# Last stage of a graph-attention kernel: x in chunks behind the first sums, VectorE's steps regrouped, the projection's bias as a matmul

## The reference, cut to what matters

```python
att = _segment_softmax(score, edge_dst, n_nodes)[..., None]      # e / (sum of e + 1e-16)
out = jax.ops.segment_sum(value * att, edge_dst, num_segments=n_nodes)
out = out.reshape(n_nodes, H * VH)
return out @ w_proj + b_proj
...
x = x + _L0_gnn_ref(h, node_vec1, edge_weight1, edge_attr_32, src, dst, batch0, ...)
```

## Time and profile before

| | us |
|---|---|
| median of 3 runs (5342.77 to 5343.44) | 5342.91 |
| the profiled execution | 5343.49 |
| its span, first to last instruction | 5341.7 |
| last stage: first DMA issued | 5205.24 |
| first "den" of VectorE | 5232.42 |
| first finish starts | 5236.56 |
| last finish starts | 5336.25 |

### The profile page before, as it was taken

The page is one execution under the profiler, slowest core; times in us unless marked ns, Lnnn a source line. Parts: engine busy times, 40 slices in busy tenths (PEclk is TensorE's granted clock), DMA queues, the critical chain, the costliest instruction groups (busy, mean ns, idle before and its releaser), DMA issues. The chain is left out here.

```text
span 5341.7 us, 120270 instructions
## 1 busy us (share of the span) xinstructions
PE 5090.1 (95%) x34849; PEld 3951.6 (74%) x34849; DVE 4194.0 (79%) x8740; ACT 2107.5 (39%) x4768; POOL 3641.1 (68%) x3589
## 2 busy tenths in 40 slices
PE   3679999999999999999999999999999999999975
PEld 3557777777777777777777777777777777777764
DVE  5647788888888788888878888887888888887877
ACT  1434444444444444444443434444344444444421
POOL 2467777777777777777777777777777777777715
PEclk8689999999999999999999999999999999999965
DMA  5566676766667676766667676666767666676735
GB/s 148 149 168 188 183 191 181 192 183 188 189 182 191 179 194 183 190 187 185 187 182 192 181 192 187 187 187 183 191 180 194 184 189 187 183 191 183 191 70 145
DMA packets 1076171, 963.37 MB, mean 180 GB/s; under 512 B 188372, under 2 KB 911096, under 8 KB 1075199
## 3 DMA queue, kind: packets, MB, share of 16 engines
q1 hardware_dynamic: 945211, 716.69, 48.5%
q0 software_dynamic: 108784, 223.44, 16.4%
q10 hardware_dynamic: 21524, 15.49, 1.1%
HBM read 809.06 MB, written 149.13 MB: 179 GB/s over the span
## 5 line engine op out<-in xcount | busy, mean ns | idle before, releaser
L1037 POOL DMA_INDIRECT gath<-msg_src,idx x3328 | 3467.7, 1042 | 1361.3 <-issue 1016.7
L1184 ACT ACTIVATE h<-z_ps,b 128x256 f32<-128x256 f32 x832 | 394.7, 474 | 1853.4 <-PE z_ps L1242 1825.2
L1223 ACT ACTIVATE sil<-a_ps,ba 128x512 f32<-128x512 f32 x832 | 572.9, 689 | 981.0 <-PE a_ps L1339 962.2
L1283 PE MATMUL rad_ps<-wval,hot 128*128 128x136 f32 x6656 | 935.5, 285 | 23.1 <-DVE run L1145 23.0
L1344 PEld LDWEIGHTS v_ps<-wv,msgT 128*128 128x128 f32 x6656 | 874.7, 192 | 43.7 <-issue 0.5
L1339 PE MATMUL a_ps<-msgT,wa 128*128 128x512 f32 x1664 | 890.3, 617 | 8.7 <-DVE msgT L1155 8.6
L1344 PE MATMUL v_ps<-wv,msgT 128*128 128x128 f32 x6656 | 878.0, 275 | 0.0
L1283 PEld LDWEIGHTS rad_ps<-wval,hot 128*128 128x128 f32 x6656 | 852.2, 195 | 30.8 <-issue 30.7
L1111 DVE SCALAR_TENSOR_TENSOR rads<-rad_ps,b,ea_bc 128x512 f32<-128x512 f32 x832 | 624.4, 751 | 292.3 <-PE rad_ps L1257 285.1
L1155 DVE TENSOR_TENSOR msgT<-xT_ps,rads 128x512 f32<-128x512 f32 x832 | 575.7, 692 | 317.2 <-PE xT_ps L1323 297.4
L1167 DVE SCALAR_TENSOR_TENSOR sil<-a_ps,sil 128x512 f32<-128x512 f32 x832 | 571.7, 687 | 304.0 <-ACT sil L1223 289.6
(11 more groups left out here) (229 smaller groups left out, 4629.7 us busy)
## 6 DMA issues: line engine op xcount, KB each, us to landing
ea_bc<-ea_rows SPq DMA_DIRECT2D x832, 256.0 KB
win<-msg_dst SPq DMA_DIRECT2D x1664, 96.0 KB
sums<-run SPq DMA_DIRECT2D x832, 136.0 KB
rel_bc<-rel_rows SPq DMA_DIRECT2D x832, 128.0 KB
attr<-in_edge_attr_t SPq DMA_DIRECT2D x1664, 32.0 KB
gath<-msg_src,idx POOLq DMA_INDIRECT x3328
msg_dst<-dst_parts SPq DMA_DIRECT2D x98, 96.0 KB, 1.8
pen_g<-pen_rows SPq DMA_DIRECT2D x208, 32.1 KB
```

The source lines that it names most:

```text
L1037: pool.indirect_dma_start(gath[:, u, s], None, msg_src, bass.IndirectOffsetOnAxis(ap=idx[:, j // 8, at:at + 1], axis=0)).then_inc(s_gath[u ...
L1223: act.activation(sil[:, j % 8], a_ps[:, :], ACT.Silu, bias=ba[:, :]).then_inc(s_sil, 1)
L1283: last = pe.matmul(rad_ps[:, i, CE:CE + AW], lhsT=hot[:, j % 2, s], rhs=wval[:, j % 2, s].rearrange("p h k -> p (h k)"), start=(r == 0), s ...
```

## The change

Four things change in the last stage.

1. x is loaded in chunks between the sums: chunk 0 by SyncE's queue behind the sums of pairs 0 and 1, chunk c (1 to 6) by ScalarE's queue in its iteration q = 7(c - 1), behind the sums of pair q + 4 and ahead of the copy of pair q. Each group of loads uses one of three semaphores in turn.
2. VectorE's whole-chunk add of `bproj` goes, and with it the semaphore `rows_biased`. GpSimd's first add of a chunk waits for the chunk's load instead.
3. The projection's bias is added by TensorE: for each half of a pair one more matmul, a row of ones (1x128) times `bproj[0:1, :]` (1x128), starts the sum in PSUM that the projection ends.
4. VectorE's steps are regrouped. Iteration q now does den(q + 2), reciprocal(q + 1), mean(q) and share(q), finish(q - 2). The semaphore `mean_steps` counts two steps a pair, `reciprocal_steps` the other two. So the sums of pair q + 2 are wanted in iteration q.

```diff
@@ -1363,34 +1363,30 @@
             rows_x = tb("rows_x", [P, NB, C])
...
             den, share = tb("den", [P, S, 2, H]), tb("share", [P, S, 2])
+            ones_row = tb("ones_row", [1, P])
...
             s_in = [ts(f"sums_in{u}") for u in range(S)]
             s_x = [ts(f"rows_in{n}") for n in range(3)]
-            s_mean, s_T, s_Ts, s_mm, s_fin = ts("mean_steps"), ts("meanT_done"), ts("meanT_copied"), ts("projected"), ts("out_ready")
-            s_xb, s_bias, s_bw, s_out = ts("rows_biased"), ts("biases_added"), ts("bias_projected"), ts("out_stored")
-
-            def x_group(c):
-
-                return (0, 16) if c == 0 else (1, 32) if c < 3 else (2, 80)
+            s_inv, s_mean = ts("reciprocal_steps"), ts("mean_steps")
+            s_T, s_Ts, s_mm, s_fin = ts("meanT_done"), ts("meanT_copied"), ts("projected"), ts("out_ready")
+            s_bias, s_bw, s_out = ts("biases_added"), ts("bias_projected"), ts("out_stored")
 
             def load_x(eng, c):
                 if c < NB // CH - 1:
-                    eng.dma_start(rows_x[:, CH * c:CH * (c + 1)], x[P * CH * c:P * CH * (c + 1), :].rearrange("(b p) c -> p b c", p=P)).then_inc(s_x[x_group(c)[0]], 16)
+                    eng.dma_start(rows_x[:, CH * c:CH * (c + 1)], x[P * CH * c:P * CH * (c + 1), :].rearrange("(b p) c -> p b c", p=P)).then_inc(s_x[c % 3], 16)
                 else:
-                    eng.dma_start(rows_x[:, CH * c:NB - 1], x[P * CH * c:P * (NB - 1), :].rearrange("(b p) c -> p b c", p=P)).then_inc(s_x[2], 16)
-                    eng.dma_start(rows_x[0:tail, NB - 1], x[P * (NB - 1):N, :]).then_inc(s_x[2], 16)
+                    eng.dma_start(rows_x[:, CH * c:NB - 1], x[P * CH * c:P * (NB - 1), :].rearrange("(b p) c -> p b c", p=P)).then_inc(s_x[c % 3], 16)
+                    eng.dma_start(rows_x[0:tail, NB - 1], x[P * (NB - 1):N, :]).then_inc(s_x[c % 3], 16)
 
             def load_sums(eng, q, i):
                 u = q % S
                 last = eng.value_load(last_item[0:1, 2 * q + i:2 * q + i + 1], min_val=0, max_val=NI - 1)
-                need(eng, s_mean, 4 * (q - S + 1))
+                need(eng, s_mean, 2 * (q - S + 1))
                 eng.dma_start(agg[:, u, i].rearrange("p h k -> p (h k)"), sums[bass.ds(last, 1)].rearrange("o p c -> p (o c)")).then_inc(s_in[u], 16)
 
             @block.sync
             def _(sp):
-                load_x(sp, 0)
-
                 def store(c):
                     sp.wait_ge(s_fin, CH // 2 * (c + 1))
                     if c < NB // CH - 1:
@@ -1400,6 +1396,8 @@
                         sp.dma_start(out[P * (NB - 1):N, :], rows_x[0:tail, NB - 1]).then_inc(s_out, 16)
                 for q in range(NP):
                     load_sums(sp, q, 0)
+                    if q == 1:
+                        load_x(sp, 0)
                     if q % S == S - 2 and q > S:
                         store(q // S - 1)
                 store(NB // CH - 1)
@@ -1407,33 +1405,47 @@
 
             @block.gpsimd
             def _(pool):
-                pool.wait_ge(s_bw, 4)
+                pool.wait_ge(s_bw, 6)
                 for q in range(NP):
                     pair = rows_x[:, 2 * q:2 * q + 2]
-                    pool.wait_ge(s_mean, 4 * q + 4)
+                    pool.wait_ge(s_mean, 2 * q + 2)
                     pool.tensor_tensor(shared[:, q % 2], bias_out[:, :].unsqueeze(1).broadcast_to((P, 2, C)),
                                        share[:, q % S].unsqueeze(2).broadcast_to((P, 2, C)), ALU.mult).then_inc(s_bias, 1)
                     pool.wait_ge(s_bias, 2 * q + 1)
-                    pool.wait_ge(s_xb, q // (CH // 2) + 1)
+                    if q % (CH // 2) == 0:
+                        c = q // (CH // 2)
+                        pool.wait_ge(s_x[c % 3], 16 * (c // 3 + 1) if c < NB // CH - 1 else 16 * (c // 3 + 2))
                     pool.tensor_tensor(pair, pair, shared[:, q % 2], ALU.add).then_inc(s_bias, 1)
 
             @block.vector
             def _(dve):
-                dve.memset(rows_x[:, NB - 1], 0.0)
+                dve.memset(rows_x[:, NB - 1], 0.0).then_inc(s_bw, 1)
+                dve.memset(ones_row[:, :], 1.0).then_inc(s_bw, 1)
                 dve.tensor_copy(bias_in[:, :, :], bval[:, :, 1, :]).then_inc(s_bw, 1)
-                dve.wait_ge(s_bw, 3)
+                dve.wait_ge(s_bw, 5)
                 dve.tensor_copy(bias_out[:, :], PS[4][:, 0:C]).then_inc(s_bw, 1)
+
+                def den_at(q):
+                    return 2 * q if q > 1 else q + 1
+
+                def inverse_at(q):
+                    return 2 * q + 3 if q < NP - 1 else 2 * NP
+
+                def guard_den(q):
+                    dve.wait_ge(s_in[q % S], 32 * (q // S + 1))
+                    dve.tensor_scalar(den[:, q % S], agg[:, q % S, :, :, AH], 1e-16, None, ALU.add).then_inc(s_inv, 1)
+
+                def invert(q):
+                    dve.wait_ge(s_inv, den_at(q))
+                    dve.reciprocal(den[:, q % S], den[:, q % S]).then_inc(s_inv, 1)
 
                 def divide(q):
                     u = q % S
-                    dve.wait_ge(s_in[u], 32 * (q // S + 1))
+                    dve.wait_ge(s_inv, inverse_at(q))
                     need(dve, s_T, q - S + 1)
-                    dve.tensor_scalar(den[:, u], agg[:, u, :, :, AH], 1e-16, None, ALU.add).then_inc(s_mean, 1)
-                    dve.wait_ge(s_mean, 4 * q + 1)
-                    dve.reciprocal(den[:, u], den[:, u]).then_inc(s_mean, 1)
-                    dve.wait_ge(s_mean, 4 * q + 2)
                     dve.tensor_tensor(mean[:, u].rearrange("p i (h k) -> p (i h) k", h=H), agg[:, u, :, :, 0:AH].rearrange("p i h k -> p (i h) k"),
                                       den[:, u].rearrange("p i h -> p (i h)").unsqueeze(2).broadcast_to((P, 2 * H, AH)), ALU.mult).then_inc(s_mean, 1)
+                    need(dve, s_bias, 2 * (q - S) + 1)
                     dve.tensor_tensor(share[:, u], agg[:, u, :, 0, AH], den[:, u, :, 0], ALU.mult).then_inc(s_mean, 1)
 
                 def finish(q):
@@ -1442,12 +1454,14 @@
                     dve.wait_ge(s_bias, 2 * q + 2)
                     dve.tensor_tensor(pair, PS[2 + q % 2][:, 0:2 * C], pair, ALU.add).then_inc(s_fin, 1)
 
+                guard_den(0)
+                guard_den(1)
+                invert(0)
                 for q in range(NP):
-                    if q % (CH // 2) == 0:
-                        c = q // (CH // 2)
-                        chunk = rows_x[:, CH * c:CH * (c + 1)]
-                        dve.wait_ge(s_x[x_group(c)[0]], x_group(c)[1])
-                        dve.tensor_tensor(chunk, chunk, bproj[:, :].unsqueeze(1).broadcast_to((P, CH, C)), ALU.add).then_inc(s_xb, 1)
+                    if q + 2 < NP:
+                        guard_den(q + 2)
+                    if q + 1 < NP:
+                        invert(q + 1)
                     divide(q)
                     if q > 1:
                         finish(q - 2)
@@ -1456,28 +1470,30 @@
 
             @block.scalar
             def _(act):
-                act.wait_ge(s_bw, 2)
+                act.wait_ge(s_bw, 4)
                 act.activation(bias_t[:, :], PS[5][:, 0:P], ACT.Copy).then_inc(s_Ts, 1)
-                for c in range(1, NB // CH):
-                    load_x(act, c)
                 for q in range(4):
                     load_sums(act, q, 1)
                 for q in range(NP):
                     if q + 4 < NP:
                         load_sums(act, q + 4, 1)
+                    c = q // (CH // 2) + 1
+                    if q % (CH // 2) == 0 and c < NB // CH:
+                        need(act, s_bias, 2 * CH // 2 * (c - 3) + 2 if c > 2 else 0)
+                        load_x(act, c)
                     act.wait_ge(s_T, q + 1)
                     need(act, s_mm, q - S + 1)
                     act.activation(meanT[:, q % S].rearrange("p i c -> p (i c)"), PS[q % 2][:, 0:2 * P], ACT.Copy).then_inc(s_Ts, 1)
 
             @block.tensor
             def _(pe):
-                pe.wait_ge(s_bw, 1)
+                pe.wait_ge(s_bw, 3)
                 pe.transpose(PS[5][:, 0:P], bias_in[:, :, :].rearrange("p h k -> p (h k)"), ident[:, :]).then_inc(s_bw, 1)
                 pe.wait_ge(s_Ts, 1)
                 pe.matmul(PS[4][:, 0:C], lhsT=bias_t[:, :], rhs=wproj[:, :], start=True, stop=True).then_inc(s_bw, 1)
 
                 def turn(q):
-                    pe.wait_ge(s_mean, 4 * q + 3)
+                    pe.wait_ge(s_mean, 2 * q + 1)
                     need(pe, s_Ts, q if q > 1 else 0)
                     for i in range(2):
                         last = pe.transpose(PS[q % 2][:, i * P:(i + 1) * P], mean[:, q % S, i], ident[:, :])
@@ -1487,7 +1503,8 @@
                     pe.wait_ge(s_Ts, q + 2)
                     need(pe, s_fin, q - 1)
                     for i in range(2):
-                        last = pe.matmul(PS[2 + q % 2][:, i * C:(i + 1) * C], lhsT=meanT[:, q % S, i], rhs=wproj[:, :], start=True, stop=True)
```

(2 more changed lines are left out.)

## The result

The changed kernel takes **5382.5 us** (median of 4 runs, 5380.8 to 5385.1) against 5342.8 us before: ratio 1.0078, 95% interval 1.0066 to 1.0090. It is 40 us slower, where 14 us less were forecast, and outside the range.

The account below looks back on a forecast made before the run. Bound: VectorE and GpSimd taking turns, 1.85 us a pair, after a start waiting on loads. -12.9 - 16.8 + 0 + 2.4 + 1.0 + 12 = -14.3 us from 5343.49 gives 5329.2, median 5328.6; range 5312 to 5343.

Parts of the forecast that it names:

- Chunk adds: VectorE's whole-chunk bias adds go: 2.15 us saved at each of the 6 chunks behind chunk 0, -12.9 us.
- Start: Start of the last stage: first finish at about 5219.8 instead of 5236.56, behind sums 2, -16.8 us.
- Regrouping: VectorE's reordered steps: about 0.2 us a pair of its own work saved but hidden behind GpSimd, 0 us.
- Late sums: Sums wanted two pairs earlier, beside x and stores: den waits at pairs 13, 20, 27 and so on, +12 us.
- rival 2: TensorE stays at the half clock: every pair costs 2.66 us, late sums are covered, about 5352 us; chance 0.08.
- Tail: Behind the last mean, project(47) and project(48) are each 0.53 us longer, +1.0 us.
- Bias on TensorE: Two more fp32 matmuls per pair: 3 pairs at 2.66 us before the full clock holds at 1.33, +2.4 us.

Follow-up runs that it names:

- The best version: Changed kernel with one 128-row, 256-column bias matmul per pair, ScalarE's sums six pairs ahead, stores two pairs later, x loads moved: 5303.6 us, ratio 0.9927.

## Why the prediction was wrong

**Chunk adds, -12.9.** The 4.0 us intervals went, as forecast. Alone it is worth 10.3 us (5328.6 against 5318.3), since part of the adds' time had covered late sums.

**Start, -16.8.** Right in size and mechanism: -16.4, with sums 2 in use 5.5 us after their issue, behind chunk 0.

**Regrouping, 0.** Off by a little. I saw that the mean would be ready within 0.06 us of GpSimd's add and gave the turn to GpSimd; the mean gets it. I also wrote that it would make no difference then (1.84), having let the add end 0.4 later. It ends 0.25 later, the share ends with it, and the interval is 1.76: -4 to -6 us. The engines' taking turns, on which this rested, is what the rows show. The Trainium skill's rule (VectorE: DVE Perf Modes, on the DRAIN) that a semaphore costs nothing extra is not tested by any run here, since VectorE's own work was never the bound; the gain came by the order of the two engines, which the rule is silent on.

**Late sums, +12.** Right in size where it can be seen, 12.4 us in the run without bias matmul, and at the pairs that were named (13, 20, 27 and so on). But the forecast had one wait there, and from pair 13 to 41 there are two, at the pair before as well, besides one at pair 5 that it did not have; that the sum agrees is partly luck. In the changed kernel itself it is 0, as rival 2 said, because 3.32 us intervals cover it.

**Tail, +1.0.** The last two intervals took 6.2 us instead of 1.7, for the same reason as all the others: they too waited for TensorE.

**Bias on TensorE, +2.4.** This is the step that failed, twice: a cost that the term put at nothing, and a clock that it had rising after 3 pairs.

First the price of a pair. I took 0.27 us for a pass at the half clock from two starts 1.09 us apart. TensorE was not back to back there: its next transposes waited for this mean, which ended at 5236.03, and started at 5236.09.

```profile
5235.47 0.56 DVE L1435 TENSOR_TENSOR mean<-agg,den 128x256 f32<-128x256 f32 x1
```

A pass costs 0.215 us. That error alone made the pair too dear (2.66; all of one height, 2.15). Against it stands a cost that no row had: 4 steps between unlike heights at 0.29 us, 1.17 us a pair. I had priced a one-row weight load by its duration (308 ns, and the profile after has 308 for it too), and by duration it is right. What it costs is the overlap: it does not start beside the matmul in flight. The Trainium skill (TensorE: Matmul & The Clock Gate, on what each phase is for) says that weight loads are pulled ahead where the row groups do not conflict or where they go to a background buffer, and that the row count does not matter to a load's timing. The traces agree with the second sentence: 308 ns for one row, 310 for 128. On the first they show what it leaves open: a load of the same height as the matmul in flight was pulled ahead of it by 0.21 us, one of another height was not.

Then the clock. I took "no idle time at all" for what raises it. By the profile TensorE had none from the first finish on, for 158 us, and stayed at 0.50.

Together they make the interval TensorE's 3.32 instead of GpSimd's 1.76 to 1.85: 47 x 1.47 us = 69 us against the forecast's interval of 1.85. That is more than the net loss of 40 us, since the gains from the start and the chunk adds came. The two parts can be told apart by an estimate from measured intervals. The unlike steps are 47 x 1.17 = 55 us of the 69. With them gone and the clock still at the half, the interval would be 2.15 and the time about 5331 us, 12 us under the kernel before, if the sums are not late; the low clock alone is the other 14. So the step that I had put at nothing is the larger part. What the unlike steps cost in this stage at the full clock, no run shows.

I gave the slow clock 0.08 as rival 2, and gave it the wrong price, 2.66: at that price it would have been 5352. The same sum with 3.32 gives 5236.56 - 16.8 + 47 x 3.32 + 2.9 + 5.5 + 1.8 = 5386, against 5380.8 for the profiled execution, whose edge stage was 5.6 us shorter.

What should have warned me: the one row of evidence for a held full clock was of full-height matmuls only, while 20 us at 0.50 with TensorE busy for 15 said that this stage does not raise the clock easily. I laid that to the idle gaps of the chunk adds; the run without chunk adds and bias matmuls has none of them, only the waits for sums, and stood at 0.50 for 60 us at a time.

## What to carry to other kernels

Before adding a small matmul between large ones, ask what height it has: give it the full 128 rows (1/128 in each, or zeros below the first row). That took the same number of instructions and columns, and here it was the difference between 5382 and 5322 us. (One wide bias matmul instead of two ran only together with other moves; its own worth is not known.) When a stage is bound by two engines that take turns, move the instruction that decides which goes first, and look for the wait that takes over; when loads are wanted earlier, look at which bulk transfers they share the time with: issuing them sooner alone gained nothing here, issuing them sooner and moving x and the stores took the waits away.

## What the hardware showed that I had not expected

- A step between a 128-row fp32 matmul and a 1-row or 64-row one costs 0.29 us at the half clock; between equal heights it costs nothing. With 0, 2 and 4 such steps a pair took 2.13, 2.73 and 3.32 us.
- Four kernels with one-row bias matmuls (in turn with the projection, the same in the kernel before, grouped, 512 columns wide) and one with 64-row ones stayed at the half clock for 129 us or more with TensorE reported 100% busy. With 128 rows, even with 127 of them zero, the clock went to 1.0 within about 3 us of the first finish. In the edge stage 64-row matmuls stand among 128-row ones at the full clock.
- The best version kept the clock at 1.0 through its steady part with TensorE busy 15 of 20 us; the kernel before, busy 15 of 20, mostly had 0.50. PE's busy share is thus no guide to the clock.
- GpSimd's add beside VectorE's mean takes 0.72 or 0.97 us and the mean 0.73 or 0.35, by whichever starts first within 0.3 us.
